# Bias adds behind KT_lo, row norms ahead of the second norm, h2f written outside the v phase, clipped squares behind v_lo

## The reference, cut to what matters

```python
h = relu(layernorm(x))                              # x: 128 graphs, 128 nodes, 512 features
z_l, z_g, v = h @ W_lang.T, h @ W_grav.T, h @ W_V.T
A_l = relu(zn @ zn.T) * not_eye                     # zn: rows of z_l over their norms
A_g = exp(-|z_g[n] - z_g[m]|^2 / (2 sigma^2)) * not_eye
K = w_l * rownorm(A_l * adj) + (1 - w_l) * rownorm(A_g * adj)
x = x + (K @ v) @ W_O.T
h2 = relu(layernorm(x))
x = x + einsum('bnf,nm->bmf', h2, adj * adj) + bias
```

## Time and profile before

| | us |
|---|---|
| median of 3 runs | 1308.35 |
| lowest and highest | 1306.39, 1311.26 |
| the profiled execution's own time | 1311.04 |
| its span | 1309.3 |
| TensorE, VectorE, ScalarE, GpSimd busy | 1211.5, 1135.8, 702.8, 636.1 |

### The profile page before, as it was taken

How to read it: one execution, slowest core, us unless ns; L and a number is a source line. 1 busy time by engine, 2 the same in 40 slices (tenths; PEclk the granted TensorE clock), 3 DMA queues, 4 the chain that set the end, 5 groups by cost and what they waited for, 6 DMA issues and landing times.

```text
span 1309.3 us, 22837 instructions
## 1 busy us (share of the span) xinstructions
PE 1211.5 (93%) x5968; PEld 1004.8 (77%) x5968; DVE 1135.8 (87%) x1919; ACT 702.8 (54%) x1326; POOL 636.1 (49%) x988
## 2 busy tenths in 40 slices
PE   7998999999999999999999999999999999999997
PEld 7887777877777877777877777777777777777785
DVE  6687889988889988889988889898888998888878
ACT  6346555456545456545456545555545555555544
POOL 2104465555465454465555455555455545456442
PEclk9999999999999999999999999999999999999998
DMA  7242444555444554444555444455454455454322
GB/s 267 68 150 90 141 148 145 159 176 162 135 146 141 161 176 157 138 148 141 162 176 166 130 149 147 152 176 169 135 149 146 147 176 177 134 153 147 108 76 97
DMA packets 182417, 193.85 MB, mean 148 GB/s; under 512 B 20353, under 2 KB 131585, under 8 KB 182401
## 3 DMA queue, kind: packets, MB, share of 16 engines
q1 hardware_dynamic: 181824, 193.33, 47.6%
q10 hardware_dynamic: 576, 0.33, 0.1%
HBM read 103.09 MB, written 90.50 MB: 148 GB/s over the span
## 4 chain that ended last, share of the span: by engine, by line
issue 47%; POOL 37%; PE 6%; DVE 5%; DMA 2%; POOLq 2%; ACT 1%; SPq 0%; DVEq 0%; ACTq 0%
POOL x_ring L383 14%; POOL h_lo L398 7%; POOL ln L373 5%; PE ring L1027 3%; POOL rn L404 2%; POOL ln L367 2%; POOL ln L366 2%; PE ring L1118 1%; POOL ln L371 1%; POOL ln L365 1%; PE p_ps L1096 1%; POOL ln L362 1%; PE ring L1145 1%; POOL ln L369 1%; POOL ln L363 1%
## 5 line engine op out<-in xcount | busy, mean ns | idle before, releaser
L398 POOL TENSOR_TENSOR h_lo<-h2f,h_hi 128x512 fp32r<-128x512 f32 x124 | 157.6, 1306 | 285.9 <-ACT h_hi L575 285.8
L1027 PE MATMUL ring<-hT_hi,Lw_hi 128*128 128x512 f32 x640 | 252.6, 395 | 38.8 <-DVE hT_lo L680 36.1
L1027 PE MATMUL ring<-hT_hi,Lw_lo 128*128 128x512 f32 x640 | 249.2, 389 | 0.0
L1027 PE MATMUL ring<-hT_lo,Lw_hi 128*128 128x512 f32 x640 | 249.2, 389 | 0.0
L1118 PE MATMUL ring<-MT_hi,hT_hi 128*128 128x512 f32 x512 | 203.2, 397 | 11.0 <-DVE v_lo L660 11.0
L1118 PE MATMUL ring<-MT_lo,hT_hi 128*128 128x512 f32 x512 | 200.0, 391 | 0.0
L1118 PE MATMUL ring<-MT_hi,hT_lo 128*128 128x512 f32 x512 | 199.4, 389 | 0.0
L383 POOL TENSOR_TENSOR x_ring<-x_ring,bias_sb 128x512 f32 (+1 forms) x120 | 190.8, 1619 | 0.0
L540 ACT ACTIVATE v_hi<-ring 128x512 fp32r<-128x512 f32 x128 | 75.9, 593 | 206.3 <-PE ring L1118 126.0
L660 DVE TENSOR_TENSOR y_lo<-ring,y_hi 128x512 fp32r<-128x512 f32 x256 | 166.5, 680 | 15.0 <-ACT y_hi L497 14.9
L1027 PEld LDWEIGHTS ring<-hT_hi,Lw_hi 128*128 128x128 f32 x640 | 120.1, 188 | 75.9 <-DVE v_lo L660 45.4
(11 more groups left out here) (187 smaller groups left out, 2612.6 us busy)
## 6 DMA issues: line engine op xcount, KB each, us to landing
x_ring<-in_x SPq DMA_DIRECT2D x32, 1024.0 KB, 5.2
out<-x_ring SPq DMA_DIRECT2D x128, 256.0 KB, 2.6
h_dram<-h SPq DMA_DIRECT2D x62, 512.0 KB, 3.4
h_turned<-h_dram SPq DMA_DIRECT2D x248, 128.0 KB, 3.3
p_dram<-chain SPq DMA_DIRECT2D x62, 256.0 KB, 2.2
h<-p_dram SPq DMA_DIRECT2D x248, 64.0 KB, 2.7
rn_cols<-rn_dram SPq DMA_DIRECT2D x31, 256.0 KB, 4.0
k_dram<-chain SPq DMA_DIRECT2D x31, 256.0 KB, 2.0
```

Of the source, the lines that this page charges most:

```text
L398: pool.tensor_tensor(h2[1][:, b], h2f[:, b], h2[0][:, b].bitcast(F32), ALU.subtract)\
L1027: mm = pe.matmul(out, lhsT, rhs, start=(k == 0), stop=(k == len(terms) - 1))
```

## The change

On GpSimd the bias adds of group i-2 wait for KT_lo of group i-1 (`kt_split`); two of them run, then the row norms of group i, then the other two, then the second norm. On ScalarE `h2_full` leaves the v phase of one iteration and goes to the next one: graphs 0 and 1 behind the third y_hi, graphs 2 and 3 between the `h2_copy` of graphs 0 and 1 and that of graphs 2 and 3. On VectorE the clipping of the squares goes behind `v_lo(0)`, save in the first and the last group.

```diff
@@ pool: iteration
                 if lag:
                     for b in range(GB):
                         h2_lo(i - 2, b)
-                    for b in range(GB):
-                        add_bias(i - 2, b)
+
+                    pool.wait_ge(kt_split, i)
+                    add_bias(i - 2, 0)
+                    add_bias(i - 2, 1)
+                row_norms(i)
+                if lag:
+                    add_bias(i - 2, 2)
+                    add_bias(i - 2, 3)
                 if before and after:
                     norm2(i - 1)
-                row_norms(i)
@@ act: iteration, among the y_hi copies
+                        if lag and n == 3:
+                            h2_full(i - 2, 0)
+                            h2_full(i - 2, 1)
                         if before and n == 3:
                             exponentials(i - 1)
@@ act: iteration, behind them
                 if lag:
-                    for b in range(GB):
-                        h2_copy(i - 2, b)
+                    h2_copy(i - 2, 0)
+                    h2_copy(i - 2, 1)
+                    h2_full(i - 2, 2)
+                    h2_full(i - 2, 3)
+                    h2_copy(i - 2, 2)
+                    h2_copy(i - 2, 3)
@@ act: iteration, v phase
-                    if before and after:
-                        for k in ({0: [], 1: [], 2: [0], 3: [1, 2, 3]} if lag else {0: [], 1: [], 2: [], 3: [0, 1, 2, 3]})[b]:
-                            h2_full(i - 1, k)
@@ dve: iteration
                     squares(i, 1)
                     v_lo(0)
+                    clipped_squares(i)
                     add(i - 1, 0, n + 1)
@@ dve: squares
-                if q == 1:
-                    dve.wait_ge(sq_ready, 3 * g + 2)
-                    dve.tensor_scalar(sqc[:, :], sq[:, :, 0], EPS * EPS, None, ALU.max).then_inc(sq_ready, 1)
+
+            def clipped_squares(g):
+                dve.wait_ge(sq_ready, 3 * g + 2)
+                dve.tensor_scalar(sqc[:, :], sq[:, :, 0], EPS * EPS, None, ALU.max).then_inc(sq_ready, 1)
@@ dve: squared_norms and last_chain
+                clipped_squares(g)
```

## The result

The changed kernel takes 1213.97 us (median; 1213.74 to 1214.76) where the kernel before takes 1308.45 (1306.39 to 1311.26): a ratio of 0.9278, 95% interval 0.926 to 0.9296. That is 94 us less, 7 more than forecast. The profiled execution took 1213.74 us with a span of 1212.0.

What follows compares the result with a forecast made beforehand. TensorE was taken as the floor, 35.7 us of a 39.1 us iteration, with three waits and their restarts losing 3.4; saving 3.1 x 28 = 87 us from 1311.04, less 2.7 for the profiled execution, gave 1221 us, range 1211 to 1255.

Steps and rivals of the forecast that it cites:

- The floor and what is left: TensorE, per iteration: 35.7 us of work without a stall, against a period of 39.1; 0.3 of the lost 3.4 stays.
- KT_lo at 0.69, done by 2.15 to 2.5: VectorE, us after v of graph 0 starts: KT_lo ends before K v needs it at 2.72; 1.01 us stall goes.
- The blocked diagonal and v_lo(0) at 5.4, wanted at 5.44: VectorE: a GpSimd add delays the second diagonal to 4.1; v_lo(0) still ends in time, 0.38 us stall nearly gone.
- The last hT_lo at 16.2, wanted 16.3: VectorE, before the next y: with h2_full out of the v phase, the 1.20 us stall goes but for 0 to 0.2.
- row_norms earlier: GpSimd and SyncE: norms at 5.65 to 6.95, so p's part-1 store follows its turn at about 13.9; called needed.
- the K chain: From p's store and fetch through the sums to KT_hi: must be 3.4 us shorter, like the period.
- The waits say to whom: TensorE's waits per iteration: hT_lo 1.20, KT_lo 1.01, v_lo 0.38, together 2.59 us; slower restarts make the other 0.8.
- The clipping behind `v_lo(0)`, "0.17 to 0.43 us": VectorE: the moved clipping delays the four adds of K v by this much, their banks not wanted before 8 us.
- VectorE as the bound: Rival: VectorE, 33.7 busy of a 35.7 us period, adds 1 us of stalls at v_lo and hT_lo; 1241 us, chance 0.18.
- The moved contention: Rival: a late `h2_lo` blocks KT_lo as the add did, its 1.01 + 0.27 us stay; 1249 us, chance 0.12.
- The K round trip: Rival: p lands no earlier, KT_hi comes late, TensorE waits before K v; 1308 us (0.04), or slower, 1317 (0.04).

Runs made afterwards that it cites:

- h2f back: The changed kernel with h2_full put back into the v phase on ScalarE, against the kernel before: ratio 0.9582, period 37.40 us.
- the four single parts: Each on the kernel before: wait on kt_split alone 0.990; h2_full moved alone 0.9988; row norms early alone 0.9719; clipping behind v_lo(0) alone 1.024.

## Why the prediction was right, and where its working failed
- **The floor and what is left.** 132 matmuls of 0.227 us and 5.75 us of p, 35.7 us, held: the period is 35.88. I left 0.3 us an iteration over the floor; 0.15 to 0.2 was left. In the profiles the first diagonals of iterations 2 and 30 are 1095.53 us apart before and 1005.39 (126.05 to 1131.44) after, so the 28 iterations gave 90.1 us for the 87 forecast. The profiled execution as a whole lost 97.3: the other 7.2 come from the first and last groups, which I had put at nothing. The median fell by less, since I took off the 2.7 us by which the profiled execution before lay above its median, and the changed one's does not lie above: 7 us high in the end.
- **KT_lo at 0.69, done by 2.15 to 2.5.** It runs 1.35 to 2.04 after the start of v. Right, 0.1 early.
- **The blocked diagonal and v_lo(0) at 5.4, wanted at 5.44.** v_lo(0) ends at 5.46 and v of graph 1 starts at 5.51. The diagonal took 0.23 us more than the 1.35 I had from its readiness to its end, and ended at 4.13 for 4.1. The rule of the Trainium skill (SBUF — State Buffer, "Who interferes with whom") gave this step, and for GpSimd's 128x512 adds the trace agrees: what is issued under an add ends with it or one own length behind it. For its small instructions it doesn't: 31 hT_lo of the kernel before, with two inputs in SBUF, start while GpSimd is in a power of 128x4 (1.01 to 1.04 us), and take 0.67 to 0.69 us as ever.
- **The last hT_lo at 16.2, wanted 16.3.** In the trace it ends at 644.78, 16.09 after 628.69, and y starts at 16.55. Right. With h2f back, TensorE waits 38.4 us for it.
- **row_norms earlier.** The forecast said "This is needed" and that the K chain must shorten with the period, which is so, but gave the step no price and named no wait of TensorE with it. It is the part without which the others give nothing: 1.0064 without it.
- **The step that failed is the first reading.** "The waits say to whom" took three waits for three causes, 1.20, 1.01 and 0.38 us, to be added up. They were one loop's slack, put down wherever the loop met TensorE. The total came out right since all parts together cut the loop and clear the next bound, so that TensorE's own work, which was sized right, set the time. That the change had the one part in it that the sum priced at nothing is luck, as far as my working goes. For any subset the sum would have been wrong, as the four single parts show: three of them missed in size and the clipping in sign.
- **The clipping behind `v_lo(0)`, "0.17 to 0.43 us".** True only while no add runs there; under one it takes 1.19. In the changed kernel it takes 0.16.
- **The rivals.** VectorE as the bound didn't come: TensorE has 0.3 us of waits left in its like iterations, for v_lo, and its own work is 35.7 us of the period of 35.88. The moved contention didn't come: `h2_lo` ends at 629.40, 0.7 after the start of v as worked out, but does block the first diagonal (1.15 us), which had room. The K round trip, to which I gave 0.04 and 0.04, is what happens when the norms stay late, and its place was SyncE's queue, as that rival said.

## What to carry to other kernels
Before adding up an engine's waits, follow one round of the work from an instruction to itself in the next iteration; if the hand-overs on it have waiters, its length is likely the period, and only what shortens or cuts it pays. Look in it for an instruction that is short, early ready and late in its queue (here 1.2 us of norms behind a second norm that waited for something else, with eight fetches queued behind them on another engine). And judge a part of such a change beside the others: one that costs 32 us alone gave 9 to 12 in company, another went from 1.5 to 40.

## What the runs showed of the hardware that I had not expected
- A VectorE `tensor_scalar` of 128x4, 0.16 us by itself, took 1.19 us when issued behind the start of a GpSimd add, and ended with it (659.23 against 659.20). How long it takes is set by the other engine's instruction, not by its own size.
- With the clipping alone, TensorE waits 2.3 us ahead of each y, and its granted clock falls to half, from 2.4 to 1.2 GHz, in some of the iterations. In the windows below the columns are the length, then busy time of TensorE, its loads, VectorE, ScalarE and GpSimd, then the granted clock, the DMA share and GB/s:
```profile
668.00:672.00 4.00, 1.71 (x8) 1.09 (x8) 2.36 (x4) 3.11 (x5) 3.60 (x11) 1.00 0.22 72
672.00:676.00 4.00, 4.00 (x12) 3.12 (x11) 3.19 (x6) 2.02 (x4) 1.47 (x4) 0.57 0.72 162
676.00:680.00 4.00, 4.00 (x20) 3.27 (x19) 3.04 (x5) 2.06 (x4) 1.54 (x1) 1.00 0.80 291
```
  TensorE stood for 2.29 of 4 us, and in the 4 us behind that 12 matmuls ran where 20 ran in the next. Over that run the clock was 0.973; with waits of 1.2 to 1.5 us, as in the kernel before, it was 0.997. The iterations, from K v to K v, can be parted by it. Two neighbours, with the same columns:
```profile
615.38:655.25 39.87, 36.49 (x181) 30.30 (x181) 35.20 (x59) 21.39 (x40) 20.30 (x32) 1.00 0.49 151
655.25:695.85 40.60, 38.12 (x181) 31.43 (x181) 35.87 (x59) 21.80 (x40) 20.52 (x32) 0.96 0.50 157
```
  Of the 29 iterations from 131.46 to 1302.52 us, 19 have a mean clock of 0.96 and last 40.62 us in the median (40.48 to 40.75); the 10 at full clock last 39.94 (39.78 to 40.38). So an estimated 19 x 0.68 = 13 of this run's 32 us go with the lower clock, and 19 are the clipping's own.
